# Message stage of a graph network on one Trainium2 core: each mask of an epoch's attributes as four VectorE instructions over four tiles, in place of one over sixteen

## What is computed

```python
def fctp_messages(x, e, W1, W2, W3, W4):
    xs, xv = _split(x, MUL0_N, MUL1_N)          # 64 scalars, 32 vectors of 3
    es, ev = _split(e, MUL0_E, MUL1_E)          # 8 scalars, 8 vectors of 3
    s1 = jnp.einsum('ea,eb,abc->ec', xs, es, W1) * ...
    s2 = jnp.einsum('eai,ebi,abc->ec', xv, ev, W2) * ...
    v1 = jnp.einsum('ea,ebi,abc->eci', xs, ev, W3) * ...
    v2 = jnp.einsum('eai,eb,abc->eci', xv, es, W4) * ...
    ...
tp = fctp_messages(node_features[col], edge_attr_tensor, W1, W2, W3, W4)
messages = tp @ Wm + bm
agg = jax.ops.segment_sum(messages, row, num_segments=N_NODES)
upd = jnp.concatenate([node_features, agg], axis=-1) @ Wu + bu
return node_features + upd
```

## Time and profile before

| | us |
|---|---|
| median of 3 runs | 5148.68 |
| lowest and highest | 5144.36 to 5158.56 |
| span of the profiled execution | 5150.1 |
| message stage on GpSimd, first to last indirect DMA | 169.3 to 2506.9 |

### The profile page before, as it was taken

How to read it: one execution, slowest core, us unless ns; L and a number is a source line. 1 busy time by engine, 2 the same in 40 slices (tenths; PEclk the granted TensorE clock), 3 DMA queues, 4 the chain that set the end, 5 groups by cost and what they waited for, 6 DMA issues and landing times. The chain is left out here.

```text
span 5150.1 us, 109355 instructions
## 1 busy us (share of the span) xinstructions
PE 3823.2 (74%) x32221; PEld 3014.2 (59%) x32221; DVE 3980.5 (77%) x7022; ACT 1201.2 (23%) x3380; POOL 3394.2 (66%) x3256
## 2 busy tenths in 40 slices
PE   4777777777777777777699985766777777777776
PEld 3555555555555555555699984555555555555554
DVE  9998888888888888766588856777777777777776
ACT  1333333333233233333100040111211111121111
POOL 0677777777777777777400036777777777777775
PEclk8777777777778778777899997888888888888887
DMA  5343433443434433433599933333333333333332
GB/s 169 92 110 98 109 100 98 103 105 99 107 98 104 105 99 101 105 101 102 187 303 302 302 117 70 76 76 76 76 76 76 78 76 76 76 75 76 75 78 55
DMA packets 585263, 567.65 MB, mean 110 GB/s; under 512 B 180293, under 2 KB 473638, under 8 KB 584854
## 3 DMA queue, kind: packets, MB, share of 16 engines
q0 software_dynamic: 150528, 258.71, 18.9%
q1 hardware_dynamic: 401238, 230.91, 18.1%
q10 hardware_dynamic: 33408, 76.99, 4.7%
HBM read 407.78 MB, written 158.52 MB: 110 GB/s over the span
## 5 line engine op out<-in xcount | busy, mean ns | idle before, releaser
L1060 POOL DMA_INDIRECT messages<-stage,place x1568 | 1796.7, 1146 | 572.7 <-issue 449.1
L2912 POOL DMA_INDIRECT q_fg<-f,q_index x1568 | 1530.1, 976 | 491.5 <-issue 464.8
L1356 PEld LDWEIGHTS ps_m<-by_attr,turned 128*128 128x128 f32 x6272 | 1065.1, 221 | 171.3 <-issue 159.1
L1356 PE MATMUL ps_m<-by_attr,turned 128*128 128x160 f32 x6272 | 1128.0, 342 | 11.7 <-ACT stage L1270 11.7
L3166 PE MATMUL q_ps_m<-q_prod,q_onehot_sh 128*32 128x160 f32 x12544 | 659.1, 364 | 369.0 <-DVE q_sums L2974 369.0
L1324 PE MATMUL ps_y<-w_xy,xt 32*128 32x256 f32 (+3 forms) x1176 | 517.5, 759 | 541.6 <-ACT xz L1241 533.2
L3166 PEld LDWEIGHTS q_ps_m<-q_prod,q_onehot_sh 128*32 128x32 f32 x12544 | 437.1, 131 | 504.0 <-DVE q_sums L2974 361.0
L1143 DVE STREAM_TRANSPOSE turned<-masked 128x2048 f32<-128x2048 f32 x196 | 453.0, 2311 | 314.6 <-PE ps_m L1356 309.2
L1324 PEld LDWEIGHTS ps_y<-w_xy,xt 32*128 32x128 f32 (+1 forms) x1176 | 152.0, 239 | 777.6 <-ACT xz L1241 555.8
L2974 DVE SCALAR_TENSOR_TENSOR q_sums<-q_ps_m,split_q,q_sums 128x161 f32 x784 | 301.5, 385 | 356.8 <-issue 287.9
L1149 DVE STREAM_TRANSPOSE by_attr<-by_node 128x2048 f32<-128x2048 f32 (+1 forms) x294 | 547.8, 1915 | 3.0 <-ACT by_node L1244 3.0
(11 more groups left out here) (263 smaller groups left out, 3886.9 us busy)
## 6 DMA issues: line engine op xcount, KB each, us to landing
nat<-in_edge_attr SPq DMA_DIRECT2D x392, 256.0 KB
rows_in<-messages ACTq DMA_DIRECT2D x208, 324.0 KB, 3.5
rows_in<-messages SPq DMA_DIRECT2D x208, 324.0 KB, 3.4
messages<-stage,place POOLq DMA_INDIRECT x1568
q_fg<-f,q_index POOLq DMA_INDIRECT x1568
q_a<-in_edge_attr SPq DMA_DIRECT2D x196, 64.0 KB, 2.1
messages<-zeros SPq DMA_DIRECT2D x25, 324.0 KB, 3.1
xw<-in_x SPq DMA_DIRECT2D x98, 80.0 KB
```

The source lines that it names most:

```text
L1060: nc.gpsimd.indirect_dma_start(out=msgs, out_offset=bass.IndirectOffsetOnAxis(ap=place[:, r, k:k + 1], axis=0), in_=stage[:, r, k, :], in_ ...
L1356: last = nc.tensor.matmul(ps_m[g % BANKS][:, k % 2 * D0:k % 2 * D0 + D0], turned[:, r, half, k * P:(k + 1) * P], by_attr[:, r, k, :, half] ...
L2912: nc.gpsimd.indirect_dma_start(out=fg[:, i, place_of(v), :], out_offset=None, in_=f_tab, in_offset=bass.IndirectOffsetOnAxis(ap=index[:, i ...
```

## The change

Two constants are added, and each mask is made by four instructions on [128, 512], four tiles each, that follow one another without a wait. The comparison, the product and the tiles are the same, and so is what is written. The semaphore `s_mask` is raised once, by the fourth. Nothing else in the program differs; the instructions of TensorE, ScalarE, GpSimd and SyncE stand in the same order.

```diff
+MASK_PARTS = 4
+MASK_TILES = EP // MASK_PARTS
...
                         def masks(t, r, first=False):
                             n = t * 2 + r
                             dve.wait_ge(s_nat, n * 64 + 64)
-                            at = rel_t[:, bass.ds(n * EP, EP), :].rearrange("p t j -> p (t j)").unsqueeze(2).broadcast_to([P, EP * 4, 32])
                             for half in range(2):
                                 if not first or half:
                                     dve.wait_ge(s_turn, n * 2 + half)
-                                nc.vector.scalar_tensor_tensor(masked[:, :, :], at, quarter[:, half:half + 1], nat[:, :, :].rearrange("p t (j w) -> p (t j) w", w=32),
-                                                               ALU.is_equal, ALU.mult).then_inc(s_mask, 1)
+                                for part in range(MASK_PARTS):
+                                    tiles = slice(part * MASK_TILES, (part + 1) * MASK_TILES)
+                                    at = rel_t[:, bass.ds(n * EP + part * MASK_TILES, MASK_TILES), :].rearrange("p t j -> p (t j)")
+                                    last = nc.vector.scalar_tensor_tensor(masked[:, part * MASK_TILES * 4:(part + 1) * MASK_TILES * 4, :],
+                                                                          at.unsqueeze(2).broadcast_to([P, MASK_TILES * 4, 32]), quarter[:, half:half + 1],
+                                                                          nat[:, tiles, :].rearrange("p t (j w) -> p (t j) w", w=32), ALU.is_equal, ALU.mult)
+                                last.then_inc(s_mask, 1)
                                 dve.wait_ge(s_mask, n * 2 + (half + 1))
                                 if not first and not half:
                                     dve.wait_ge(s_msg, n * PAIRS0)
                                 nc.vector.transpose(turned[:, r, half, :], masked[:, :, :].rearrange("p t w -> p (t w)")).then_inc(s_turn, 1)
```

## The result

The changed kernel takes 4972.43 us (median of 4 runs, 4969.91 to 4975.09), against 5152.0 for the kernel before in the same measurement. The ratio is 0.9645, with a 95% interval of 0.9628 to 0.9662: 180 us or 3.6% less. The forecast was 4970. The profiled execution spans 4968.3 us, 181.8 less than the one before.

What follows compares the result with a forecast made beforehand. GpSimd's DMAs were the bound; after the change its own sum ends at 2310 and VectorE's path at 2326. Taking the later, 2506.9 - 2326 = 181 us less than 5150.1 gives 4969, forecast 4970 us; range 4930 to 5065, about 0.8.

Steps and rivals of the forecast that it cites:

- What bounds: Message stage: GpSimd's indirect DMAs bound it end to end, 1796.7 us busy and 572.7 idle, 274 us of it waiting on masks.
- (a): VectorE's masks: four parts of 0.709 us starting 0.63 apart make a mask 2.63 us, 0.28 more.
- (b): GpSimd's DMAs get their read between parts: waits of 0.40 us a mask, 77 us in place of 274.
- (c): VectorE nearly uses up its 193 us of slack, reaches the 42 pairs' end at 1988; last DMA 2326.
- (d): Loop through ScalarE freeing `stage`: 16.2 to 18 us against at least 20.4 for 16 DMAs, so it stays covered.
- Kept through all four: Rival: VectorE holds the read through all a mask's parts, 54 us more, 5203 us; chance 0.12.
- only at some borders: Rival: GpSimd gets its read at some part borders, waiting 0.9 to 1.0 us a mask, 5060 us; chance 0.10.
- The parts don't overlap: Rival: parts take 0.751 us each, a mask 3.00, VectorE is the bound, 5033 us; chance 0.09.
- Nothing changes: Rival: long pauses or DMA landings set the pace, shorter waits reappear as pauses, about 5150 us; chance 0.02.

Runs made afterwards that it cites:

- one_input: Kernel before with each mask replaced by one transpose with a single SBUF input (messages wrong, only time of use): 4891.69 us, ratio 0.9492.
- parts8: Changed kernel with each mask in eight instructions over two tiles in place of four: 5053.34 us, ratio 0.9808 to the kernel before.
- parts2: Changed kernel with each mask in two instructions over eight tiles in place of four: 4969.24 us, ratio 0.9648 to the kernel before.
- after_extra_b: Changed kernel plus an extra [128, 320] VectorE transpose after each into `turned`, on a third chip: 5017.95 us, ratio 0.9737 to the kernel before.
- before_extra: Kernel before plus an extra [128, 320] VectorE transpose after each into `turned`: 5160.1 us, ratio 1.0016.
- after_waits: Changed kernel with a semaphore wait between a mask's four parts, on a slow chip: 5762.88 us, ratio 1.0023 to the kernel before.

## Why the prediction was right

*What bounds.* It rested on the sum of GpSimd's busy and idle time over the stage, and one_input confirms it: with the waits gone, the time falls by 262 us.

*(a) VectorE's price* was put too low. A mask takes 2.74 us, not 2.63: 0.39 more than one instruction, not 0.28. The step that failed is the duration of a part. Parts take 0.746 us and start 0.66 apart; I had 0.709 and 0.63, from a [128, 128] instruction of the same operation. The overlap of 0.08 was right. By the formula of the Trainium skill, page "VectorE: DVE Perf Modes", section "The TRN2 errata — SBUF-src ops pay a fixed extra latency per instruction", a part takes 0.691 us as an estimate, which is lower still. Its 2.76 us for four is close to the measured 2.74 only because the short part and the missing overlap cancel. Its rule as to direction (each instruction pays again) holds, and parts8 shows where it wins.

*(b) GpSimd's waits* were put too high, 77 us against 39. The mechanism, a read served at each border, is shown by the rows of the changed kernel and by parts2. Mis-sized are both of its terms. Sorted by mask (with the read 0.12 us after a DMA's start), the first DMA that wants its read during one waits 24 us in all 192 masks, 0.13 a mask, where I had 0.29; those after it add 14 us, 0.07 a mask, where I had used 0.11. Both come from where the DMAs fall. I had the next DMA ask 0.02 after a border, or wait a whole part. With parts 0.66 apart, two parts are 1.33, and a DMA that asks 1.276 after it was served comes 0.05 before a border and waits only that. The mask that I showed above is such a case, and the 94 waits that end with the fourth part are 0.08 us each on average. First ones, which I had spread evenly, bunch too: 67 want their read within 0.2 us of the mask's start, and those wait for nothing. That is luck of the numbers, and not a property of four parts.

*(c) VectorE as the bound.* It was forecast to arrive at the end of the 42 pairs at 1988; it got there at about 1995, with no wait for `turned` until then. The two errors of (a) and (b) have opposite signs, but only (a) could move the result, since VectorE decided: 0.11 x 168 = 18 us later, of which 13 were in the sum for meetings that the measured 2.74 already holds. The first mask also started 3 us later (132.9 against 129.8). What followed took 334 us where I had 338, so the last DMA ended at 2329, forecast 2326, and the stages behind were 4 us shorter, where I had counted on none of that. The mechanism was right; that the forecast is within 3 us of the median is in part luck, since these small errors nearly cancel. after_extra_b shows the bound by experiment, before_extra that it had not been one.

*(d) The loop through ScalarE.* Here I looked at the wrong wait. GpSimd's new short pauses (48 of them, up to 3.3 us, 81 us in all) come in the middle of epochs, where it waits for the first four groups of the epoch after, and not at the start, which I had costed:

```profile
1195.67 0.97 POOL L1062 DMA_INDIRECT messages<-stage,place  x1 [0.30 <-issue]
1199.72 0.96 POOL L1062 DMA_INDIRECT messages<-stage,place  x1 [3.07 <-ACT stage L1276]
```

The DMA after this pause is the ninth of its epoch, and so it is for all 48 pauses. The row puts the pause down to ScalarE, but TensorE had to start these groups first, and it had stood still for 6.28 us until VectorE made `sel`, right behind `by_attr`:

```profile
1190.72 0.57 PE L1324 MATMUL ps_m<-sel,xw 128*128 128x128 f32 x1 [6.28 <-DVE sel L1163]
```

So here it is the same bound, VectorE, seen from the other end. It was not always so: between 345 and 2121 us the profile ends 34 of these waits of TensorE with `sel` and 43 with the load of `xw`, which SP issues behind its loads of `nat`; what an earlier `xw` would give was not tried. I had named pauses of 0.3 to 4 us as the sign that (c) is wrong. That sign was badly chosen: with VectorE as the bound, GpSimd has to pause. For (d) itself, each of SP's four loads of `nat` moves 256 KB by the page, not the 64 that I had given; VectorE waited for `nat` 0.3 us in all.

*The rivals.* "Kept through all four" and "only at some borders" fall with the rows of the changed kernel: DMAs end 0.84 us after each of the parts. "The parts don't overlap" falls with parts of 0.746 us that start 0.66 apart, and after_waits shows masks of 3.12 us where a wait stands between them. The prediction tied it to the rule of the Trainium skill, page "VectorE: DVE Perf Modes", section "The DRAIN you can't avoid", that the next instruction waits for the pipe to empty; the section goes on to say that one that is not held starts earlier, and that is what the rows show. "Nothing changes" falls too, on the chips where the kernel before takes 5150. On two others none of the kernels with shorter waits or none was faster, though not by this rival's mechanism; no rival of mine had instructions that reach TensorE late in it.

## What to carry to other kernels

Where GpSimd issues indirect DMAs back to back, subtract their undisturbed duration from the mean: what remains may be waits for VectorE instructions that read two tiles from SBUF. Here nearly all DMAs that had waited ended 0.84 us after such an instruction. A single SBUF input is no guarantee: the cast of line 1178 reads one tile, at 1.6 elements per ns, and the DMA under it took 1.47 us. Splitting the instruction trades the wait for VectorE time and stops paying as soon as VectorE is the bound (with eight parts 81 us were lost again); moving the smaller input to PSUM removed the wait for 0.35 us an epoch and was the better cure here. Before costing a gain on the bounding engine, sum up the next one: here 234 of 274 us of waits went, but the time fell by 180 only, because VectorE, with 193 us of slack, paid for the cut and became the bound.

## What the runs showed of the hardware that was not expected

- GpSimd's read was served between two instructions of VectorE that overlap by 0.08 us, and neither was held up for it: the 185 parts that follow a border at which a waiting read was served took 0.745 us (median), the other 403 that follow a part 0.746, and both kinds began 0.08 before the end of the one ahead.
- An instruction with two SBUF inputs paid 0.13 us each time that it is repeated back to back (parts of 512 elements, 0.533 us, start 0.66 apart; of 1024, 1.067, start 1.20 apart), against 0.07 for transposes (2048 elements, 2.133 us, start 2.20 apart).
- In the changed kernel TensorE's groups got slower. Behind its wait of 6.28 us the granted clock was 0.50 from 1190.7 to 1194.1 us and 0.76 up to 1198.8, and the epoch's groups took 2.34 and 4.68 us. In the kernel before, where TensorE had been at work since 1202.92, the clock was 1.00 and they took 1.29 and 3.63. These 2.1 us an epoch fall on the way from VectorE to GpSimd's ninth DMA.
- The long pauses of GpSimd are not a constant. They stand at the same places in every run, ahead of the second DMA behind each 112. Twelve of the thirteen are 4.8 to 6.2 us long in the kernel before (67 us in all), in the changed kernel they are 1.9 to 5.5 us (54), with two parts 0.8 to 5.2 (28). What they are was not settled.
- Chips differ: the kernel before takes 5151 to 5154 us on two of them and 5747 and 5872 on two others, where the 4.6% that the copy in PSUM gains was not to be seen. With that kernel TensorE stood still ahead of its matmuls of `ps_m` for 224 us on one of the slow chips and for 12 on a fast one; the cause is open.
